# LSTM stage of a four-layer graph kernel: the first weight product of the graph convolution from one fp32 matmul to three fp32r passes, with new merged instruction orders

## What is computed

```python
h = relu(einsum('ts,bsh->bth', adj, x @ Wg0 + bg0))
h = relu(einsum('ts,bsh->bth', adj, h @ Wg1 + bg1))
for p in range(1, 5):                      # windows of p nodes
    nw = T // p
    wins = h[:, :nw * p].reshape(B * nw, p, H)
    last = lstm_last(Wih[p-1], Whh[p-1], bih[p-1], bhh[p-1], wins)
    h = h.at[:, arange(nw) * p + (p - 1)].set(last.reshape(B, nw, H))
```

## Time and profile before

| what | value |
|---|---|
| device time, median of 3 runs | 1216.42 us (1216.35 to 1217.83) |
| the profiled execution | 1217.63 us, its span 1214.2 us |
| LSTM stage | from the start to about 652 us of the span |
| one of its turns, in the middle | about 77.9 us |
| mean granted TensorE clock | 0.991 |

### The profile page before, as it was taken

The page is one execution under the profiler, slowest core; times in us unless marked ns, Lnnn a source line. Parts: engine busy times, 40 slices in busy tenths (PEclk is TensorE's granted clock), DMA queues, the critical chain, the costliest instruction groups (busy, mean ns, idle before and its releaser), DMA issues. The chain is left out here.

```text
span 1214.2 us, 23748 instructions
## 1 busy us (share of the span) xinstructions
PE 1166.9 (96%) x7820; PEld 1021.3 (84%) x7820; DVE 988.7 (81%) x2735; ACT 811.0 (67%) x1810; POOL 413.1 (34%) x789
## 2 busy tenths in 40 slices
PE   5999999999999999999997999989999799989998
PEld 4798898998989989889896889867777688879997
DVE  5888988889888888888886999977777688876655
ACT  4785876858868688687785777757776466663332
POOL 4211100001001000010013777756665788853332
PEclk8999999999999999999998999999999899999999
DMA  8400000000000000000000000000000000002222
GB/s 259 119 1 1 1 2 0 0 0 0 0 0 0 0 0 0 0 0 1 1 2 1 1 2 2 2 1 1 1 1 1 1 2 1 2 1 62 70 74 75
DMA packets 26305, 20.83 MB, mean 17 GB/s; under 512 B 1776, under 2 KB 22256, under 8 KB 26224
## 3 DMA queue, kind: packets, MB, share of 16 engines
q1 hardware_dynamic: 25648, 19.68, 5.6%
q10 hardware_dynamic: 576, 0.13, 0.1%
HBM read 11.42 MB, written 8.39 MB: 16 GB/s over the span
## 5 line engine op out<-in xcount | busy, mean ns | idle before, releaser
L554 ACT ACTIVATE gate<-ps,b_lstm 128x256 f32<-128x256 f32 (+2 forms) x624 | 309.9, 565 | 93.8 <-PE ps L581 92.5
L579 PE MATMUL ps<-H_hi,w_hi 128*128 128x256 f32 (+2 forms) x624 | 210.3, 338 | 1.9 <-DVE H_lo L470 1.2
L580 PE MATMUL ps<-H_hi,w_lo 128*128 128x256 f32 (+2 forms) x624 | 205.0, 330 | 0.0
L581 PE MATMUL ps<-H_lo,w_hi 128*128 128x256 f32 (+2 forms) x624 | 192.8, 330 | 0.0
L131 POOL TENSOR_SCALAR rstd<-mv 128x8 f32<-128x8 f32 x16 | 5.0, 312 | 498.8 <-DVE mv L111 498.6
L579 PEld LDWEIGHTS ps<-H_hi,w_hi 128*128 128x128 f32 x624 | 117.5, 188 | 16.1 <-DVE H_lo L470 3.2
L580 PEld LDWEIGHTS ps<-H_hi,w_lo 128*128 128x128 f32 x624 | 117.7, 189 | 8.1
L581 PEld LDWEIGHTS ps<-H_lo,w_hi 128*128 128x128 f32 x624 | 115.4, 189 | 10.0 <-DVE H_lo L508 1.5
L579 PE MATMUL ps<-hid_hi,w_hi 128*128 128x256 f32 (+2 forms) x384 | 120.3, 320 | 0.3
L580 PE MATMUL ps<-hid_hi,w_lo 128*128 128x256 f32 (+2 forms) x384 | 116.6, 310 | 0.0
L561 ACT ACTIVATE tanh_c<-cell 128x512 f32<-128x512 f32 (+2 forms) x176 | 90.9, 517 | 24.4 <-DVE cell L498 17.4
(11 more groups left out here) (205 smaller groups left out, 3105.4 us busy)
## 6 DMA issues: line engine op xcount, KB each, us to landing
out<-x SPq DMA_DIRECT2D x32, 256.0 KB, 2.3
x<-in_WihT SPq DMA_DIRECT2D x1, 768.0 KB, 11.3
x<-in_WhhT SPq DMA_DIRECT2D x1, 768.0 KB, 5.9
x<-in_x_in SPq DMA_DIRECT2D x2, 256.0 KB, 3.6
x<-in_x_in SPq DMA_DIRECT2D x1, 512.0 KB, 7.9
x<-in_WihT SPq DMA_DIRECT2D x1, 256.0 KB, 8.2
tanh_c<-in_WqkvT SPq DMA_DIRECT2D x1, 192.0 KB, 4.8
w_sb<-in_W SPq DMA_DIRECT2D x1, 192.0 KB, 4.0
```

The source lines that it names most:

```text
L554: nc.scalar.activation(gate[:, g, z, 0:w * GB], gate_bank(g, k, m)[:, 0:w * GB], ACT.Tanh if z == G else ACT.Sigmoid, bias=b_lstm[:, 4 * ( ...
L579: nc.tensor.matmul(dst, w_hi[:, src, p - 1, z], v_hi, start=start, stop=False)
L580: return nc.tensor.matmul(dst, w_lo[:, src, p - 1, z], v_hi, start=False, stop=False)
L581: return nc.tensor.matmul(dst, w_hi[:, src, p - 1, z], v_lo, start=False, stop=stop)
```

## The change

`w_g[:, 0]` is split once, in the first turn, into an fp32r high half (ScalarE) and a low half (VectorE). ScalarE's copy of A0 now writes the fp32r high half of the product. VectorE subtracts it from the same PSUM bank for the low half, a new part ULOW, four times a turn. W0 becomes three fp32r passes; the wait for the low half stands right ahead of the third. For k = 0 the two halves live in `hid_hi` and `hid_lo`, for k = 1 in new tiles. All three orders are new. Nine tables of the last layer are allocated behind the LSTM stage's scope, and `moved` and `ones_r` lie in `H_lo` and `H_hi`.

```diff
-        VECTOR_PARTS = by_chunk(OUT, W0, U1, A1)
+        VECTOR_PARTS = by_chunk(OUT) + [(q, c, 0) for c in range(CH) for q in (ULOW, W0)] + by_chunk(U1, A1)
...
-        ON_TENSOR = ("BBBaaaaBBBaBBbabbababaabbaababbaaabbbbbaaaaaabaaaabbbbabbbbbbaaaabaaaaaaaabbaaabbaaabbabbbbababb"
-                     "bababbbbaaaaaaaaabbbbbaabbaaaabbaaabbbabbabaaabbbb")
-        ON_VECTOR = ("saassstaBBBastssbtsbaastbaatbbttbaabbaaabatbbabaabbaabbbaabbataabbaabaabbaaaabbabbaabbbbaabaabba"
-                     "aabbabbaabbabb")
-        ON_SCALAR = ("aaBBBBBbbaaaaaabbaaaabbbsbbaabaabbsaaabbbbsaabbbsaaaasbbaaaatbbabbsaaaaabbbtbaabttaabbbbbaaaasbb"
-                     "abbtstaaaaabbbbtbaaabbbbaatb")
+        ON_TENSOR = ("aaaBBaBBBBBaBbbabbaabaabbaaabbbaaabbbbbaaaaaabaaaabbbbbabbbbbaaaabaaaaaaaabbbbaaaaaaabbbbbbbbaa"
+                     "bbbaabbbbaaaaaaaaabbbaabbbaaababbaaabbaaababbbbbbba")
+        ON_VECTOR = ("ataaBBaaBsabbbaasbtbaatbsssbsssababbaasababtabababbaabttbbaabbattaabbaabaabbaataabbbabaabbbbaab"
+                     "aabbaaaabbbbaabbabb")
+        ON_SCALAR = ("aBBBaBBbbaaaaaabbaaaabbbbaaaabbbbaaabbbbaabbbaaaabbaaasabbabbsaaaaabbbbbaaabbbttbbaaaatbbassbb"
+                     "saaaaasbbbbbssaaatbbbaabbtttt")
...
+                dve.wait_ge(S["o_split"], 1)
+                nc.vector.tensor_tensor(w_g0_lo[:], w_g[:, 0], w_g0_hi[:].bitcast(F32), ALU.subtract).then_inc(
+                    S["o_bias"], 1)
                 dve.wait_ge(S["ld_xb"], 16)
...
+                    elif what == ULOW:
+                        dve.wait_ge(sa(g, "a_ax"), i * CH + k + 1)
+                        u_hi, u_lo = product_halves(g, k)
+                        nc.vector.tensor_tensor(u_lo, ps[:, 4 * g + k], u_hi.bitcast(F32), ALU.subtract).then_inc(
+                            sa(g, "a_ulo"), 1)
...
+                act.wait_ge(S["ld_g"], n_g)
+                nc.scalar.activation(w_g0_hi[:], w_g[:, 0], ACT.Copy).then_inc(S["o_split"], 1)
...
-                        nc.scalar.activation(u[:, g, k * CB:(k + 1) * CB],
-                                             ps[:, 4 * g + k].rearrange("p (b t) -> p b t", b=CB),
-                                             ACT.Copy).then_inc(sa(g, "a_ax"), 1)
+                        nc.scalar.activation(product_halves(g, k)[0], ps[:, 4 * g + k], ACT.Copy).then_inc(
+                            sa(g, "a_ax"), 1)
...
-                        nc.tensor.matmul(ps[:, 4 * g + 2 + k], w_g[:, 0],
-                                         u[:, g, k * CB:(k + 1) * CB].rearrange("p b t -> p (b t)"),
-                                         start=True, stop=True).then_inc(sa(g, "a_w0p"), 1)
+                        u_hi, u_lo = product_halves(g, k)
+                        nc.tensor.matmul(ps[:, 4 * g + 2 + k], w_g0_hi[:], u_hi, start=True, stop=False)
+                        nc.tensor.matmul(ps[:, 4 * g + 2 + k], w_g0_lo[:], u_hi, start=False, stop=False)
+                        pe.wait_ge(sa(g, "a_ulo"), i * CH + k + 1)
+                        nc.tensor.matmul(ps[:, 4 * g + 2 + k], w_g0_hi[:], u_lo, start=False, stop=True).then_inc(
+                            sa(g, "a_w0p"), 1)
```

More of the change, by code:

```diff
@@ L78, in four_layers @@
         iota_p = sb("iota_p", [P, EC])
[L79 to L87, removed]
         adj_sb = sb("adj_sb", [P, P])
@@ L114, in four_layers @@
         A = [sync_names(nc, ctx, " ".join(f"{n}{g}" for n in
-                                          "a_stats a_aggr a_scale a_shift a_hn a_axp a_ax a_w0p a_w0 a_up a_u a_Hp a_H a_gatep "
+                                          "a_stats a_aggr a_scale a_shift a_hn a_axp a_ax a_ulo a_w0p a_w0 a_up a_u a_Hp a_H a_gatep "
                                           "a_gate a_Hlo a_part a_cell a_tanh a_hid a_h32 a_lo a_outp a_out".split()))
@@ L162, in four_layers @@
         S = sync_names(nc, ctx, "ld_e ld_x0 ld_xa ld_adj ld_g ld_xb ld_w ld_w1 ld_lstm ld_late ld_x1 ld_x pool_made w_high "
-                                "w_low pool_link dve_link o_scale o_shift o_bias o_moved o_taken b_made o_products")
+                                "w_low pool_link dve_link o_scale o_shift o_bias o_moved o_taken o_split o_products")
         RAW = 6 * NB
@@ L189, in four_layers @@
         hid_lo = tmp0("hid_lo", [P, 2, 512], F32R)
+        u1_hi = tmp0("u1_hi", [P, 2, 512], F32R)
+        u1_lo = tmp0("u1_lo", [P, 2, 512], F32R)
+        w_g0_hi = tmp0("w_g0_hi", [P, P], F32R)
+        w_g0_lo = tmp0("w_g0_lo", [P, P], F32R)
         gate = tmp0("gate", [P, 2, 4, 512])
@@ L193, in four_layers, with product_halves @@
         tanh_c = tmp0("tanh_c", [P, 2, 512])
-        moved = hid_hi[:].rearrange("p k (c e) -> p k c e", c=EC)
-        ones_r = hid_lo[:, 0, 0:P]
+        def product_halves(g, k):
+            return (hid_hi[:, g], hid_lo[:, g]) if k == 0 else (u1_hi[:, g], u1_lo[:, g])
+        moved = H_lo[:, 1].rearrange("p t b -> p (t b)").rearrange("p (k c e) -> p k c e", k=2, c=EC)
+        ones_r = H_hi[:, 1].rearrange("p t b -> p (t b)")[:, 0:P]
         key_row, is_less, ends_rowf = hid[:, 0, 0:E], hid[:, 0, E:2 * E], hid[:, 1, 0:E]
@@ L213, in four_layers @@
         TG, TP = gates_before[NS], parts_before[NS]
-        A0, OUT, W0, U1, A1, SHARE, HIGH, LOW, REST, GATE, KEEP, CELL, TANH, HIDDEN, STATS, AGGR, APPLY = range(17)
+        A0, OUT, ULOW, W0, U1, A1, SHARE, HIGH, LOW, REST, GATE, KEEP, CELL, TANH, HIDDEN, STATS, AGGR, APPLY = range(18)
         def recurrent(k):
@@ L432, in part @@
                         nc.vector.tensor_tensor(add1[:], ps[:, 7, P:2 * P], b1_bc[:], ALU.add).then_inc(S["o_bias"], 1)
-                        dve.wait_ge(S["o_bias"], 3)
+                        dve.wait_ge(S["o_bias"], 4)
                     turn_part(i, g, what, k, m, before)
@@ L438, in part @@
                         dve.wait_ge(S["ld_lstm"], n_lstm)
-                        nc.vector.tensor_tensor(b_lstm[:], b_ih[:], b_hh[:], ALU.add).then_inc(S["b_made"], 1)
+                        nc.vector.tensor_tensor(b_lstm[:], b_ih[:], b_hh[:], ALU.add).then_inc(S["o_bias"], 1)
                     if opening(i) and (what, k, g) == (A1, 1, 0):
@@ L531, in part @@
                     if opening(i) and (what, k, m) == (GATE, 0, 0):
-                        act.wait_ge(S["b_made"], 1)
+                        act.wait_ge(S["o_bias"], 5)
                     if opening(i) and (what, k, g) == (TANH, NS - 1, 0):
@@ L589, in part @@
                         pe.wait_ge(S["ld_g"], n_g)
-                        pe.wait_ge(S["o_bias"], 2)
+                        pe.wait_ge(S["o_bias"], 3)
                         nc.tensor.matmul(ps[:, 7, P:2 * P], b0_part[:], w_g[:, 1], start=True, stop=True).then_inc(
@@ L593, in part @@
                     if opening(i) and (what, k, g) == (W0, 1, 1):
-                        pe.wait_ge(S["o_bias"], 3)
+                        pe.wait_ge(S["o_bias"], 4)
                     if opening(i) and what in (SHARE, HIGH):
@@ L680, in four_layers @@
         part0.close()
+        hot_s = sb("hot_s", [P, E])
+        hot_d = sb("hot_d", [P, E], F32R)
+        hot_sd = sb("hot_sd", [P, E], F32R)
+        hot_sT = sb("hot_sT", [P, EC, P])
+        hot_dT = sb("hot_dT", [P, EC, P])
+        same = sb("same", [P, EC, E])
+        cut_f = sb("cut_f", [P, E])
+        cut_b = sb("cut_b", [P, E])
+        log_a = sb("log_a", [P, EC])
         part, tmp = scope()
```

1 line of the change is left out of this document (added).

## The result

The changed kernel takes **1226.14 us** (median of 4 runs, 1225.96 to 1228.02), the kernel before in the same measurement 1216.96 (4 runs, 1216.35 to 1217.83). The ratio is 1.0075, with a 95% interval of 1.0056 to 1.0094: 9.2 us slower, where 4.3 us faster was forecast.

The account below looks back on a forecast made before the run. The prediction took TensorE to bound the LSTM stage. Its terms, -5.4 (W0) - 0.5 (waits) + 0.7 (opening) + 0.9 (end) = -4.3 us, gave a forecast of 1212.0 us, own range 1209.5 to 1214.5, with rivals 1208.0 to 1217.0.

Parts of the forecast that it names:

- W0 on TensorE: LSTM stage: three fp32r passes take 0.69 us against 0.86 for one fp32 product; 32 products save 5.4 us.
- ULOW on VectorE: Four subtractions a turn, 2.4 to 2.7 us, hidden in VectorE's 10.1 us of idle time.
- no waits at the third pass: W0's last pass: TensorE's waits for ULOW's low halves should be rare and under 0.1 us; 0.3 us would mean Rival 3.
- The loss per turn is some 0.2 us where the old order lost up to 0.4: TensorE's waits in each LSTM turn under the new orders; counted as 0.5 us of gain over the stage.
- behind step 3 the orders are nearly the same: Later part of each turn: argued against new orders removing the old waits, the largest of which, for `hid_lo`, are there.
- just fits: Turn's start: a's OUT.0 comes 1.78 us behind a's last gate product; VectorE has the hidden state by 1.58.
- The opening: Stretch up to the first gate product, bound by VectorE: 0.7 us of loss, between 0 and 2.5.
- The end: Last turn: a's hidden state is uncovered, transposes wait about 1.7 us for `H`; 0.9 us lost once, 0 to 1.7.
- Rival 3: VectorE bounds each turn's first 23 us, TensorE waiting for ULOW at the third pass; some 4 us slower, 1221; chance 0.09.
- Rival 2: Waits of 0.3 to 0.4 us per turn at W0.1's third pass or ahead of A1; 1214 to 1217 us; chance 0.19.
- rival 4: LSTM stage: weight loads bound it, a product costs three loads, not two; 6.1 us slower, 1222.5; chance 0.03.

Follow-up runs that it names:

- Experiment 1: Kernel before with the three new orders alone: ULOW does nothing, W0 stays one fp32 matmul; 1228.71 us, ratio 1.0073.
- experiment 9: Changed kernel with Experiment 4's edit, plus a's last step and b's step 9 exchanged on all three engines; 1223.67 us, ratio 1.0041.
- experiment 2: Changed kernel with the old TensorE and ScalarE orders and VectorE's old order with four ULOW put in; 1233.42 us, ratio 1.011.
- Experiment 4: Changed kernel with both pairs of ranking comparisons moved to the opening's first W0, where VectorE waits for data; 1220.13 us, ratio 1.0003.
- experiment 3: Changed kernel with a's last gate product moved back ahead of b's step 9 in TensorE's order only; 1224.39 us, ratio 1.0042.
- Experiment 14: Changed kernel with Experiment 4's edit, plus a's OUT parts behind b's last step in the last turn alone; 1218.69 us, ratio 0.9998.

## Why the prediction was wrong

The forecast of -4.3 us and the measured +9.2 are 13.5 us apart. At the marks of the first table, 6.6 of them lie in the six turns (-4.4 forecast, +2.2 found), and 6.9 outside them, in the opening and the last turn.

- **W0 on TensorE: right.** 0.71 us a product against 0.69 forecast. Experiment 1 against the changed kernel shows the four products' 0.63 us a turn at b's U1.0.
- **ULOW on VectorE: the amount right, the cover right by a hair.** 70.0 us busy in a turn (70.3 forecast), and no waits at the third pass in the middle turns, as said. In experiment 9, where VectorE came to a's ULOW.0 some 1 us later in the turn, the waits are there.
- **"The loss per turn is some 0.2 us where the old order lost up to 0.4" is the step that failed most.** I laid out the first 16 us of the turn and took over the remaining 62 with "behind step 3 the orders are nearly the same". The head came out at -0.38 (about -0.6 by my layout; its first 0.2 to 0.3 us go to a's OUT.0, which "just fits" and doesn't quite). The part that I had not laid out lost +0.67. Experiment 1 measures the reorder by itself: the new orders cost 0.8 us a turn, and I had priced them at a small gain. That is one way to divide the loss, as experiment 2 shows that the split without them costs more. A middle turn was forecast at 77.2 us and is 78.2.
- **The opening: 0.7 forecast (up to 2.5), 2.3 at the first gate, 3.6 at turn 1.** I counted instructions moved in and out of VectorE's chain by their durations, 2.4 against 1.9. I missed that moving the chain in time puts the ranking beside GpSimd's splits, where it takes three times as long, and no term had a lower clock, under which the first gates run. Experiment 4 shows both gone together: the 4.5 us at the first gate are about the 4.6 us of the two pairs, and the 1.1 us that turn 1 gains beyond them are what experiment 3 gains with the clock at full there.
- **The end: 0.9 forecast (0 to 1.7), 3.4 found.** The wait was as forecast (1.76 us against "about 1.7"). The rest is the clock behind the wait, which was in no term. In experiment 1, with the same orders and the same wait (1.82 us at 651.84), the granted clock stays at 1.00 and the end costs 1.8. So some 1.8 are the wait and the order, and some 1.6 the clock. That the wait is what lowers the clock isn't shown, since there it did not. In experiments 3 and 4 waits of 1.83 and 1.77 us were followed by the half clock as in the changed kernel. Experiment 14 removes the wait for a and both parts go.
- **The rivals.** Rival 3 was nearest in time (1221) and named the right engine, but not the place: the third pass is where the next microsecond would be lost, not where these were. Rival 2 had half of the saving given back; against experiment 1 the split gave back 0.13 of its 0.63 us. None said that the new orders cost more than the old ones had lost in waits, though they were the largest part of the diff, and none had the ends of the stage. With 0.12 on slower, the chances were too sure.

Still open: why the new strings fit each other less well behind the head. The places of the waits are shown, but no order was found that has the head of the new one and the rest of the old. And the executions of experiments 4 and 14 spread over 9.6 and 5.7 us, those of the changed kernel over 2.1. The spread goes with the mean granted clock (in experiment 4 from 0.996 at 1214.4 us to 0.983 at 1223.95); what sets that clock from one execution to the next is open.

## What to carry to other kernels

When a change brings new hand-written orders, price the reorder as a part of its own, over the whole period and not only where the new operations stand, and measure both halves (new orders with old operations, new operations in old orders) before crediting either: here they cost 0.8 and 1.9 us a turn alone and 0.33 together. An engine's idle sum says nothing about room at a place: here 2 us less work changed nothing and 2.4 us more at another place cost 1.65. Look apart at what happens once, at the opening and at the end: two edits there returned 9.4 us at the stage's end of the changed kernel, and 1.6 in the kernel before.

## What the runs showed of the hardware

- The same two VectorE instructions (scalar comparison, 128x256) took 0.73 us with GpSimd idle and 1.82 to 2.65 us beside GpSimd's 128x512 subtractions (12 pairs in seven traces). What an operation costs depends on when it runs.
- In the changed kernel a wait of 1.76 us on TensorE at the end of a long busy stretch was followed by the half clock (from 651.6 us), some 1.6 us more lost. In experiment 1 a wait of 1.82 us at the same place was not. In the opening, waits of 1.05 and 1.21 us were followed by 3.4 us at half clock, and in experiment 4, without them, the granted clock from 27 to 39 us is 1.00. In experiment 1 waits of 1.30 and 0.58 us at these places were followed by none (1.00 from 26 to 40). I had priced waits at their length only.
- fp32r passes of 512 columns with a new weight each start 0.23 to 0.24 us apart, mixed with fp32 work or not, with loads busy for 90% of the turn (70.64 of 78.23 us); rival 4's bound by loads does not appear.
